# Sparse layers of a macaron transformer: token lists from one-hot products, rows gathered per block, three weight buffers filled by ScalarE

## The reference, cut to what matters

```python
x = x + 0.5 * sparse(_layernorm(x))          # sparse layer 1, turn=1
x = x + attention(_layernorm(x))
x = x + 0.5 * sparse(_layernorm(x))          # sparse layer 2, turn=2
x = x + 0.5 * local_attention_block(...)     # two inner layers
x = x + retention(_layernorm(x))
x = x + 0.5 * local_attention_block(...)

def sparse(x):                               # x: 4096 tokens (16 x 256) of 128
    top1 = argmax(softmax(x @ router_w + router_b))        # 8 experts
    for i in range(8):
        a, g = split(x @ w1[i] + b1[i])                    # 512 each
        y = (a * sigmoid(g)) @ w2[i] + b2[i]
        out = out + where(top1 == i, y, 0)
```

## Time and profile before

| | |
|---|---|
| median of 3 runs | 2328.78 us (2327.08 to 2331.36) |
| the profiled execution's own time | 2330.9 us |
| its span in the profile, first to last instruction | 2329.1 us |
| mean granted TensorE clock | 0.966 |
| busy: TensorE / VectorE / ScalarE / GpSimd | 93% / 74% / 73% / 62% of the span |

### The profile page before, as it was taken

How to read it: one execution, slowest core, us unless ns; L and a number is a source line. 1 busy time by engine, 2 the same in 40 slices (tenths; PEclk the granted TensorE clock), 3 DMA queues, 4 the chain that set the end, 5 groups by cost and what they waited for, 6 DMA issues and landing times. The chain is left out here.

```text
span 2329.1 us, 67714 instructions
## 1 busy us (share of the span) xinstructions
PE 2169.4 (93%) x22534; PEld 1603.6 (69%) x22534; DVE 1727.4 (74%) x3644; ACT 1708.7 (73%) x6026; POOL 1453.2 (62%) x1442
## 2 busy tenths in 40 slices
PE   5697999999498999999999999899999999999999
PEld 3695666665398688874688864675788864788863
DVE  3595888886387798974799874575899973899964
ACT  3354888886254899983899983555899983899982
POOL 4573777774575588870688870472688860788850
PEclk8898899999699999999999999999999999999999
DMA  6111000000112100000000000000000000000000
GB/s 244 46 48 48 2 0 0 0 0 6 49 47 96 42 10 9 7 3 5 9 7 9 9 1 0 2 0 5 9 7 9 9 1 5 9 9 7 9 1 36
DMA packets 34266, 47.46 MB, mean 20 GB/s; under 512 B 6384, under 2 KB 27760, under 8 KB 33744
## 3 DMA queue, kind: packets, MB, share of 16 engines
q1 hardware_dynamic: 29584, 36.38, 5.3%
q0 software_dynamic: 4544, 9.35, 1.3%
HBM read 24.38 MB, written 12.96 MB: 16 GB/s over the span
## 5 line engine op out<-in xcount | busy, mean ns | idle before, releaser
L279 POOL TENSOR_TENSOR space<-space 128x512 f32<-128x512 f32 x256 | 324.8, 1269 | 271.9 <-DVE space L382 271.6
L274 POOL TENSOR_TENSOR space<-space 128x512 f32<-128x512 f32 x256 | 267.1, 1043 | 127.1 <-ACT space L315 126.7
L329 ACT ACTIVATE space<-psum,space 128x128 f32<-128x128 f32 x1024 | 336.4, 386 | 2.2 <-DVE space L373 2.2
L176 PE MATMUL psum<-big,space 128*128 128x256 f32 x1024 | 267.1, 383 | 7.9 <-issue 4.6
L1010 POOL TENSOR_TENSOR space<-space 128x256 f32<-128x256 f32 (+1 forms) x256 | 221.0, 884 | 85.3 <-DVE space L1112 83.2
L268 POOL TENSOR_TENSOR space<-space 128x512 f32<-128x512 f32 x256 | 266.3, 1040 | 7.9 <-DVE space L353 7.0
L373 DVE TENSOR_REDUCE space<-psum 128x4 f32<-128x512 f32 x256 | 177.1, 692 | 100.8 <-PE psum L191 96.3
L1056 ACT ACTIVATE space<-psum,space 128x128 f32<-128x128 f32 (+1 forms) x512 | 209.7, 442 | 1.7 <-DVE space L1105 1.7
L329 ACT ACTIVATION_READ_ACCUMULATOR space<-psum,space 128x1 f32 x1024 | 203.2, 198 | 0.0
L176 PEld LDWEIGHTS psum<-big,space 128*128 128x128 f32 x1024 | 175.0, 191 | 30.2 <-issue 16.9
L208 PE MATMUL psum<-space 64*64 64x128 f32 (+2 forms) x4096 | 174.9, 275 | 7.0 <-ACT space L300 7.0
(11 more groups left out here) (191 smaller groups left out, 5453.5 us busy)
## 6 DMA issues: line engine op xcount, KB each, us to landing
big<-early SPq DMA_DIRECT2D x1, 6944.0 KB
space<-sorted_x SPq DMA_DIRECT2D x78, 64.5 KB
z<-token_y SPq DMA_DIRECT2D x16, 256.0 KB, 5.8
space<-z SPq DMA_DIRECT2D x64, 64.0 KB, 1.9
space<-z SPq DMA_DIRECT2D x64, 63.8 KB, 2.0
big<-late SPq DMA_DIRECT2D x1, 3114.0 KB, 13.7
x<-x_t SPq DMA_DIRECT2D x4, 512.0 KB, 5.3
x_final<-x SPq DMA_DIRECT2D x8, 256.0 KB, 2.0
```

What stands on the lines that cost most here:

```text
L176: ins = mm(qk_ps[:, t * T:(t + 1) * T].rearrange("p (n c) -> p n c", n=2), hT[:, k, t * P:(t + 1) * P], wq[:, 0:2, j, :], start=(t == 0), ...
L274: pool.tensor_tensor(x, x, rn[:, (j - 1) % 2, :].unsqueeze(2).to_broadcast([P, 8, LD]), ALU.mult).then_inc(scaled, 1)
L279: pool.tensor_tensor(t3[:, j % 2, :], t1[:, j % 2, :], t2[:, j % 2, :], ALU.add).then_inc(summed, 1)
L329: ins = act.activation(pr[:, j % 2, h, t * P:(t + 1) * P], s_ps[h][:, t * P:(t + 1) * P], ACT.Exp, bias=nm[:, j % 2, h, t:t + 1], accum_ou ...
```

## The change

Rows are no longer sent to a sorted copy. SP stores each unit's `xt` to `rows` in DRAM in token order (row = partition * 32 + tile), and TensorE makes the list of the token numbers of each block:

- `place(n)` also splits the place within the expert's list into a whole number of blocks (`whole`) and the row in the block (`low`).
- `first_blocks()` works out each expert's first block from the counts; with it `high` is each token's block.
- `in_row` is a bf16 one-hot of `low` (128 wide a tile; GpSimd makes 24 tiles of it during the routing, VectorE the last 8), `in_block` a bf16 one-hot of `high` (39 wide a tile).
- `counted` is `in_block` times the token's partition part (ScalarE) and times one more than its tile (GpSimd). 32 bf16 products of `in_row` with `counted`, summed in one PSUM bank, give for every row of every block its token's number plus 1, or 0 where there is none: `ids` and, with spare rows for the empty ones, `targets`.
- In `experts` GpSimd gathers a block's rows from `rows` by an indirect DMA (four buffers), and scatters the result of the block seven before. The up weights are copied by ScalarE, behind the sigmoids, to one of three buffers. SP has nothing to do there.

```diff
     def sync(sp):
         if begin is not None:
             loads(sp)
-        sp.wait_ge(stop_ready, ONE + 1)
-        for e in range(EX):
-            at = sp.value_load(stop[0:1, e:e + 1], min_val=0, max_val=EX * REGION)
-            sp.dma_start(g.sorted_x[ds(at, P), :], g.spare_rows[:, e, :]).then_inc(g.spared, 16)
-        sp.wait_ge(g.spared, 16 * (EX * turn + 1))
+        rows = g.rows.rearrange("(p t) c -> p t c", t=TILES)
+        for u in range(U):
+            sp.wait_ge(xt_ready, S0 + u + 1)
+            sp.dma_start(rows[:, PER * u:PER * (u + 1), :], xt[:, PER * u:PER * (u + 1), :]).then_inc(g.rows_stored, 16)
...
+                if n == LAST:
+                    pe.wait_ge(taken_ready, G0 + LAST + 1)
+                    mm(count_ps, g.ones, taken[:, LAST + 1, :], start=True, stop=True, skip_group_check=True).then_inc(count_ready, 1)
...
-        pe.wait_ge(taken_ready, G0 + len(GROUPS))
-        pe.wait_ge(rank_read, G0 + len(GROUPS))
-        mm(rank_ps[:, 0, :], g.ones, taken[:, len(GROUPS), :], start=True, stop=True, skip_group_check=True).then_inc(stop_ps, 1)
+        for t in range(TILES):
+            if t % CHUNK == 0:
+                pe.wait_ge(by_row, ONE * (TILES // CHUNK) + t // CHUNK + 1)
+                pe.wait_ge(by_tile, ONE * (TILES // CHUNK) + t // CHUNK + 1)
...
+            ins = mm(id_ps, in_row[:, t, :], counted[:, t, :, :], start=(t == 0), stop=(t == TILES - 1), skip_group_check=True)
+        ins.then_inc(ids_ps, 1)
...
+        for c in range(TILES // CHUNK):
+            act.wait_ge(in_block_ready, ONE * (TILES // CHUNK) + c + 1)
+            ts = slice(c * CHUNK, (c + 1) * CHUNK)
+            act.activation(counted[:, ts, 0, :], in_block[:, ts, :], ACT.Copy, scale=g.row_of[:, 0:1]).then_inc(by_row, 1)
...
-            link(dve.reduce_sum(pos[:, 0:k], total[:, 0:k, :], AX.X))
-            dve.tensor_copy(g.place[:, t0:t1], pos[:, 0:k]).then_inc(place_ready, 1)
-            dve.wait_ge(place_ready, G0 + n + 1)
+            link(dve.reduce_sum(pos[:, t0:t1], total[:, 0:k, :], AX.X))
+            link(dve.tensor_copy(whole_i[:, t0:t1], pos[:, t0:t1]))
+            link(dve.tensor_scalar(whole_i[:, t0:t1], whole_i[:, t0:t1], 7, None, ALU.arith_shift_right))
+            link(dve.tensor_copy(whole[:, t0:t1], whole_i[:, t0:t1]))
+            dve.scalar_tensor_tensor(low[:, t0:t1], whole[:, t0:t1], -float(P), pos[:, t0:t1], ALU.mult, ALU.add).then_inc(low_ready, 1)
...
-        for n, (u0, u1) in enumerate(GROUPS):
-            pool.wait_ge(place_ready, G0 + n + 1)
+        for n, (u0, u1) in enumerate(GROUPS[:LAST]):
+            pool.wait_ge(low_ready, G0 + n + 1)
+            pool.wait_ge(logits_ready, S0 + u1)
             for t in range(PER * u0, PER * u1):
-                pool.wait_ge(xt_ready, S0 + t // PER + 1)
-                pool.indirect_dma_start(out=g.sorted_x, out_offset=bass.IndirectOffsetOnAxis(ap=g.place[:, t:t + 1], axis=0),
-                                        in_=xt[:, t, :], in_offset=None).then_inc(g.sent, 16)
+                pool.tensor_scalar(in_row[:, t, :], g.row_in_block, low[:, t:t + 1], None, ALU.is_equal).then_inc(row_ready, 1)
+        for c in range(TILES // CHUNK):
+            ts = slice(c * CHUNK, (c + 1) * CHUNK)
+            pool.wait_ge(in_block_ready, ONE * (TILES // CHUNK) + c + 1)
+            pool.tensor_tensor(counted[:, ts, 1, :], in_block[:, ts, :], g.tile_of[:, ts].unsqueeze(2).to_broadcast([P, CHUNK, BLOCKS]), ALU.mult).then_inc(by_tile, 1)
...
     def gpsimd(pool):
-        prev.there(pool, 0)
-        if turn == 1:
-            pool.wait_ge(g.early_there, 16)
-        for s in range(BLOCKS + 4):
+        listed(pool)
+        pool.wait_ge(g.rows_stored, 16 * U * turn)
+        for s in range(BLOCKS + LAG):
             if s < BLOCKS:
-                e = expert_of(pool, s)
-                if s >= 2:
-                    pool.wait_ge(y_ready, S0 + s - 1)
-                pool.tensor_copy(w_up[s % 2], g.l0_w1[:, ds(e * UP, UP)]).then_inc(up_staged, 1)
-                pool.wait_ge(up_staged, S0 + s + 1)
-            u = s - 4
+                if s >= DEEP:
+                    pool.wait_ge(xT_ps, S0 + s - DEEP + 1)
+                pool.indirect_dma_start(out=xb[:, s % DEEP, :], out_offset=None, in_=g.rows,
+                                        in_offset=bass.IndirectOffsetOnAxis(ap=g.ids[:, s:s + 1], axis=0)).then_inc(xb_ready[s % DEEP], 16)
+            u = s - LAG
...
     def scalar(act):
+        def stage(s):
+            e = expert_of(act, s)
+            if s >= 3:
+                act.wait_ge(y_ready, S0 + s - 2)
+            act.activation(w_up[s % 3], g.l0_w1[:, ds(e * UP, UP)], ACT.Copy).then_inc(up_staged, 1)
...
+            if s + 1 < BLOCKS:
+                stage(s + 1)
```

More of the change, by code:

```diff
@@ L1391 @@
 TILES = N // P
-REGION = N + P
 BLOCKS = TILES + EX - 1
@@ L1407, in norm_and_route @@
     FED = (3, 6, 8)
-    loads, spare_rows, arrived, rest_there = begin if begin is not None else (None, None, None, nothing)
+    loads, arrived, rest_there = begin if begin is not None else (None, None, nothing)
     sq, lnv, rstd = sb("sq", [P, 4, W]), sb("lnv", [P, 2, W]), sb("rstd", [P, 4, W])
@@ L1415, in norm_and_route @@
     added = sb("added", [P, EX])
[L1416 to L1422, removed]
+    total = sb("total", [P, TILES, EX])
+    pos, low, whole, high = sb("pos", [P, TILES]), sb("low", [P, TILES]), sb("whole", [P, TILES]), sb("high", [P, TILES])
@@ L1580, in vector @@
                 rest_there(dve)
-                dve.tensor_copy(xt[:, :, P].bitcast(mybir.dt.uint32), g.row_of).then_inc(id_ready, 1)
-                link(dve.tensor_copy(taken[:, 0, :], g.region))
-            if ends_with.get(s - 4) is not None:
-                place(ends_with[s - 4])
+                link(dve.memset(taken[:, 0, :], 0.0))
+            n = ends_with.get(s - 4)
+            if n is not None:
+                if n == LAST:
+                    first_blocks()
+                place(n)
@@ L1603, in vector @@
-        end = ends[e]
-        link(dve.tensor_tensor(owner[:, :, :], one(g.block_of), each(end[:, :]), ALU.is_ge))
+        link(dve.tensor_tensor(high[:, :], high[:, :], whole[:, :], ALU.add))
+        for c in range(TILES // CHUNK):
+            ts = slice(c * CHUNK, (c + 1) * CHUNK)
+            dve.tensor_tensor(in_block[:, ts, :], g.block_of.unsqueeze(1).to_broadcast([P, CHUNK, BLOCKS]),
+                              high[:, ts].unsqueeze(2).to_broadcast([P, CHUNK, BLOCKS]), ALU.is_equal).then_inc(in_block_ready, 1)
@@ L1605, in vector @@
         link(dve.reduce_sum(owned[:, :], owner[:, :, :], AX.X))
         link(dve.tensor_scalar(owned[:, :], owned[:, :], float(EX - 1), None, ALU.min))
-        dve.tensor_copy(g.block_expert[:, :], owned[:, :])
-        link(dve.tensor_scalar(full[:, :], full[:, :], -1.0, float(REGION // P), ALU.mult, ALU.add))
-        link(dve.tensor_tensor(owner[:, :, :], owner[:, :, :], each(full[:, :]), ALU.mult))
-        link(dve.reduce_sum(row[:, :], owner[:, :, :], AX.X))
-        link(dve.tensor_tensor(row[:, :], row[:, :], g.block_of, ALU.add))
@@ L1612, in vector @@
[L1612 to L1625 removed]
+        dve.tensor_copy(g.block_expert[:, :], owned[:, :]).then_inc(table_ready, 1)
```

163 lines of the change are left out of this document (86 added, 77 removed).

## The result

The changed kernel took 2312.05 us (median of 4, 2308.98 to 2314.36) where the kernel before took 2327.93 (median of 4): ratio 0.9925, 95% interval 0.9909 to 0.9941. It is faster, by 16 us. The forecast was 39 us, and 2290; the time lies inside the range of 2281 to 2319, near its top.

The account below looks back on a forecast made before the run. TensorE bounds the blocks; the seam before them waits for scatters and the first block's fetch. Seam -22.4 and -18.7, block starts +2: -39.1 us from the profiled 2330.9 or median, 2291.8 and 2289.7, called 2290; range 2281 to 2319.

Parts of the forecast that it names:

- The seam: Stretch before each sparse layer's blocks where TensorE idles: first transpose 22.4 us earlier in layer 1, 18.7 in layer 2.
- C: Start of `choose(4)`, the last group's choice in the routing: forecast 38.5 us in layer 1 and 593.4 in layer 2.
- the chain: Routing steps from the start of `choose(4)` to the first block transpose: 16.0 us, between 14.0 and 18.5.
- Reading the late signals as a cost of the scatters that goes with them: Routing: unexplained "remote" waits for TensorE (5.77, 4.93, 8.38 us) come from the scatters and vanish with them; unproven.
- TensorE's work stays the same, so the period stays 2.79: Expert blocks: TensorE remains the bound at 2.79 us a block if no other engine exceeds it.
- start of the blocks +1 a layer: Start of the blocks: table load waits for the first gate product, weight copies delay ScalarE; +1 us a layer, 0.3 to 2.
- Rival 3: Blocks: late signals move there with two indirect DMAs per 2.79 us, 0.55 us a gather; +43 us, 2333; chance 0.08.
- Rival 1: Routing: late signals stay, belonging to its small products; about -7 us, 2322; chance 0.17 with mixtures.
- Rival 2: Blocks: GpSimd or ScalarE becomes the bound; +20 us, 2310, or +23, 2313; chance 0.17.
- Rival 4: Seam before the blocks: no shorter than now, because the list's chain takes as long as the scatters; chance 0.02.
- The narrow fits: Blocks: ScalarE at 2.6 and GpSimd at 2.56 us both just fit in the 2.79 us period.
- The rule weighed: Blocks: VectorE's fp32 copy shuts GpSimd out of descriptor writing for the whole copy; forecast used the trace's 0.06 us instead.

Follow-up runs that it names:

- m: The changed kernel as it is, run again where the kernel before took 2312.51 us: 2288.50 us, ratio 0.9897, blocks of 120.8 and 120.5 us.
- c: The kernel before with only the weight part of the change (three up-weight buffers, filled by ScalarE): 2329.58 us, blocks of 120.7 and 121.0 us.
- i to l: Changed kernel with GpSimd's plain store for the scatter, more TensorE signals, gathers for every second block only, or an extra plain fetch: 2288.52, 2286.70, 2288.04, 2288.27 us.

## Why the prediction was wrong

**The seam: right.** Forecast -22.4 and -18.7, measured 76.9 to 54.71, -22.2, and -18.4 in layer 2 (counted from the start of the layer, which is now 9.3 us earlier: 628.1 to 600.45 + 9.3). C came 0.7 us before the forecast 38.5 in layer 1 and at the forecast in layer 2 (584.20 + 9.3 = 593.5), the chain 16.87 and 16.25 where 16.0 was worked out. Single terms were off and cancelled: from the first `in_block` to the end of GpSimd's last multiply it is 45.08 to 49.97, 4.9 us and not 4.5.

**Reading the late signals as a cost of the scatters that goes with them: half right, and here it failed.** They left the routing with the scatters. But "TensorE's work stays the same, so the period stays 2.79" and "start of the blocks +1 a layer" made the blocks +2 in the sum; they were +12.0 and +12.2. The failed step is the blocks' period: 2.79 us holds only if TensorE's signals are on time beside two indirect transfers in each block, and in the result they were not, so that stops made it 3.11 us in the mean of layer 1 and 3.15 in layer 2. Rival 3 named this mechanism. Its price was too high, 0.55 us a gather from the 17.5 us of the earlier trace rows over 32 scatters; measured it is 24.2 / 78 = 0.31, below the 0.50 from which it would decide, so the kernel still got faster. It also had no case in my range between "none" and "all of it"; the time fell inside the range by luck, in room made for rivals 1 and 2, which did not happen.

**The sum with its measured terms:** -22.2 - 18.4 + 12.0 + 12.2 = -16.4, and the medians differ by 15.9. (The two profiled executions differ by 19.2: the unchanged remainder was 2.8 shorter in the second.)

**In the other condition the forecast holds for the changed kernel, but not for the gain.** m takes 2288.5, forecast 2290. But before takes 2312.5 there, not 2328. Its two levels lie 15 to 22 us apart in the groups. I take that to be late signals in its routing: in the late condition VectorE waits 9.6 + 7.9 us for them in layer 2 and 8.5 in layer 1, a part of it off the path. Without a trace of before in the other condition this is argued and not shown. Read so, the lists by themselves are worth 24 us (2312.5 to 2288.5). In the condition with late signals they also save some 15 us of late signals in the routing (2327.9 to 2312.5), and pay 24 in the blocks.

**Rival 1** (late signals stay in routing): no "remote" there. **Rival 2**: ScalarE is not the bound (c: 120.7; m: 2.79 apart with all copies in place). GpSimd is not either: in m it issues both transfers in each block and still waits for the transposes. **Rival 4**: the chain is 16.9 us. **The narrow fits** held: the weight copy of ScalarE took 1.09 us (1.06 forecast), its register load stayed hidden, and m's blocks are 120.8 us against 120.6, so the +1 us at the start did not show.

**The rule weighed.** In the changed kernel a gather that started while VectorE's 0.49 us copy ran took 1.15 us; one that had a whole copy inside its span took 0.97, as long as those without one. The longest gather of the trace took 1.27, 0.30 more. In m the gather kept its 0.97, and it was VectorE's copy that took 0.70. By the Trainium skill ("SBUF — State Buffer", section "SBUF: two separate sides") GpSimd can't write descriptors while such a copy runs, and whichever of the two comes second waits for the whole of the other. The traces don't bear out a whole copy: where one of the two was longer, it was by 0.2 to 0.3 us. Whoever pays, in m it was off the path. First the changed kernel, then m:

```profile
72.83 0.49 DVE L1799 COPY hn<-big 128x640 f32 x1 [0.47 <-issue]
...
73.02 1.15 POOL L1708 DMA_INDIRECT space<-rows,ids  x1 [0.70 <-PE psum L1732]
...
76.15 0.97 POOL L1708 DMA_INDIRECT space<-rows,ids  x1 [0.68 <-remote]
76.34 0.49 DVE L1799 COPY hn<-big 128x640 f32 x1 [0.84 <-issue]
```

```profile
73.19 0.97 POOL L1708 DMA_INDIRECT space<-rows,ids  x1 [0.54 <-PE psum L1732]
...
73.76 0.70 DVE L1799 COPY hn<-big 128x640 f32 x1 [0.15 <-DVE space L1793]
```

## What to carry to other kernels

A wait whose releaser the trace can't name is a cost to be followed: ask what load brings it about, and where the change puts that load next. Here the change took the dense indirect transfers out of a stage that waited anyhow and put them beside TensorE's fullest stage, which gave back 24 of 41 us. When TensorE runs without a gap, keep to one indirect transfer of GpSimd per 2.8 us beside it and give plain ones to SyncE; here buffers one block deeper did not help. And time the kernel before in every group: without its 2310 the runs i to l would have passed for four cures.

## What the runs showed of the hardware

- In the condition with late signals, two indirect transfers of GpSimd for each 2.79 us block of TensorE bring waits of up to 2.6 us for TensorE's signals, and stops of TensorE that make the blocks 3.11 us in the mean. One is free (120.1 us). Half the rows or half the bytes of the gather make next to no difference (133.1 and 133.7 against 134.4 us in layer 2). Buffers one block deeper don't help (137.2 against 132.6), and with them TensorE stops even between products that wait for nothing.
- In four of the seven groups of runs none of it shows. The changed kernel itself ran in one of these (2288.5 us, blocks of 120.8, against 2312.05 and 132.6 in the result); the rest goes by the kernel before (2309.6 to 2312.5 against 2327 to 2332) and by variants. One chip was seen in both conditions. What sets the condition is open.
- Whether the signals are late or TensorE's products are is open too: ends of products are modelled in the trace, and the run that would load the signals alone never met the late condition.
